# Second fold of the query weights as three products of f16 parts, with scales found by two more all-reduces over the partitions, and one inverse root for the first two norms

## The reference

```python
x = x + attn(layernorm(x)); x = x + ffn(layernorm(x))
# attn: 16 heads, low-rank queries, keys and values from one latent of 64
q = (h @ Wqa) @ Wqb                  # nope part 64, rope part 64 of each head
c_kv, k_pe = split(h @ Wkva, 64)     # latent 64, rope key 64
k_nope, v = split(c_kv @ Wkvb)       # 64 and 128 of each head
scores = [q_nope, rope(q_pe)] @ [k_nope, rope(k_pe)].T / sqrt(128), causal
attn_out = (softmax(scores) @ v) @ Wo
# ffn: router softmax over 16 experts, top 2, expert width 176, plus a shared expert of width 352
```

## Time and profile before

| | us |
|---|---|
| median of 3 runs | 1742.45 (1738.38 to 1745.92) |
| the profiled execution, its own time | 1731.52 |
| its span, first to last instruction | 1729.7 |
| PE busy | 1514.9 (88%) |
| DVE busy | 1314.3 (76%) |
| ACT busy | 1027.5 (59%) |
| POOL busy | 989.7 (57%) |
| start of the first scores of tile 0 | 79.6 |

### The profile page before, as it was taken

The page is one execution under the profiler, slowest core; times in us unless marked ns, Lnnn a source line. Parts: engine busy times, 40 slices in busy tenths (PEclk is TensorE's granted clock), DMA queues, the critical chain, the costliest instruction groups (busy, mean ns, idle before and its releaser), DMA issues.

```text
span 1729.7 us, 45005 instructions
## 1 busy us (share of the span) xinstructions
PE 1514.9 (88%) x16388; PEld 1089.9 (63%) x16389; DVE 1314.3 (76%) x2967; ACT 1027.5 (59%) x2342; POOL 989.7 (57%) x1597
## 2 busy tenths in 40 slices
PE   8777989889889999998899999988999999889990
PEld 2355666666656776666567766665677666666660
DVE  2587888888778778877887788778877888555556
ACT  1365656656656666666666666666666666556660
POOL 3156764435487676556876765568766443553440
PEclk9999999999999999999999999999999999999995
DMA  6236842221363333212634332126233311347418
GB/s 181 55 89 150 151 75 43 60 55 22 68 117 66 70 63 63 55 22 63 123 66 70 62 64 55 21 62 124 63 67 55 59 32 26 89 137 228 133 41 297
DMA packets 329877, 144.41 MB, mean 83 GB/s; under 512 B 277346, under 2 KB 320389, under 8 KB 329672
## 3 DMA queue, kind: packets, MB, share of 16 engines
q1 hardware_dynamic: 304592, 105.41, 30.5%
q10 hardware_dynamic: 18168, 19.41, 3.7%
q0 software_dynamic: 6912, 16.83, 3.1%
HBM read 47.04 MB, written 29.53 MB: 44 GB/s over the span
## 4 chain that ended last, share of the span: by engine, by line
PE 48%; DVE 26%; ACT 8%; issue 5%; DMA 5%; SPq 2%; POOL 1%; ACTq 0%; DVEq 0%; POOLq 0%
PE of_ps L681 20%; PE s_ps L681 16%; PE t_ps L842 10%; DVE pT L1613 7%; DVE smax L1584 3%; ACT pT L1028 3%; DVE smax L1588 2%; DVE nmax L1595 2%; DMA qT<-work 2%; DVE smax L1566 1%; ACT probs L1155 1%; DVE work L1418 1%; DVE nmax L1592 1%; ACT probs L1160 1%; ACT work L1028 1%
## 5 line engine op out<-in xcount | busy, mean ns | idle before, releaser
L1613 DVE TENSOR_TENSOR pT<-t_ps,pT 128x512 f16<-128x512 f32 (+3 forms) x688 | 409.5, 598 | 164.0 <-ACT pT L1028 160.6
L681 PE MATMUL s_ps<-kT,qT 128*128 128x512 f16 (+3 forms) x2304 | 492.3, 328 | 12.4 <-DMA qT<-work 7.7
L1028 ACT CAST pT<-t_ps 128x512 f16<-128x512 f32 (+3 forms) x688 | 354.5, 515 | 235.1 <-PE t_ps L842 234.5
L842 PE MATMUL t_ps<-id,probs 128*128 128x128 f32 x2304 | 381.3, 280 | 74.7 <-DVE pT L1613 34.7
L842 PEld LDWEIGHTS t_ps<-id,probs 128*128 128x128 f32 x2304 | 256.9, 141 | 178.5 <-issue 90.6
L1155 ACT ACTIVATE probs<-s_ps,nmax,fac 128x640 f32<-128x640 f32 (+3 forms) x256 | 269.0, 1051 | 1.7 <-DVE nmax L1592 1.7
L681 PEld LDWEIGHTS s_ps<-kT,qT 128*128 128x128 f16 x2304 | 219.0, 99 | 80.4 <-DMA qT<-work 8.3
L681 PEld LDWEIGHTS of_ps<-ckv,pT 128*128 128x128 f16 x6912 | 241.1, 98 | 38.8 <-DVE o_sb L1447 8.8
L681 PE MATMUL of_ps<-ckv,pT 128*128 128x64 f16 x6912 | 258.3, 193 | 6.5 <-DVE o_sb L1447 6.1
L681 PE MATMUL of_ps<-weights,xT 128*128 128x512 f16 (+1 forms) x936 | 200.2, 351 | 37.0 <-DVE ks_sb L1405 19.0
L1584 DVE TENSOR_REDUCE smax<-s_ps 128x1 f32<-128x512 f32 (+1 forms) x256 | 157.2, 647 | 3.6 <-PE s_ps L681 3.2
(11 more groups left out here) (224 smaller groups left out, 2444.7 us busy)
## 6 DMA issues: line engine op xcount, KB each, us to landing
wgu_sb<-wgu ACTq DMA_DIRECT2D x8, 704.0 KB, 4.4
work<-lists SPq DMA_DIRECT2D x40, 128.5 KB
qT<-lists SPq DMA_DIRECT2D x40, 128.5 KB, 2.1
x_sb<-x SPq DMA_DIRECT2D x32, 128.0 KB, 2.4
x<-x SPq DMA_DIRECT2D x32, 128.0 KB, 2.5
dense<-den SPq DMA_DIRECT2D x32, 128.0 KB, 2.1
weights<-dense ACTq DMA_DIRECT2D x1, 4096.0 KB, 20.0
qT<-y_exp SPq DMA_DIRECT2D x16, 256.0 KB, 6.8
```

Source lines behind the costliest of these rows:

```text
L681: return pe_.matmul(o, a, b, start=start, stop=stop)
L842: last = pe_.transpose(t_ps[:, h, c * P:(c + 1) * P], probs[:, u % 2, g * L + j * P:g * L + (j + 1) * P], id32[:, :])
L1028: return act.copy(o, i)
L1613: dve.tensor_tensor(pT[:, u % 2, 1, h, 0:w], t_ps[:, h, 0:w], pT[:, u % 2, 0, h, 0:w], ALU.subtract).then_inc(s.lo_p, 1)
```

## The change

The second fold multiplies f16 parts of scaled operands. For that the scales of three operands are needed before it: of `Wqa` (A), of the rope columns (B) and of the first fold's product (C). DVE finds the largest magnitudes of A and B from the loaded weights (`fold_factors`) and of C from PSUM in two halves (`fold_products`); POOL reduces them over the partitions in two all-reduces (`fold_reduce`: A and B, then C); DVE makes the scales (`fold_scales`), ACT ten hi parts of at most 512 columns, DVE ten lo parts. Each part of the fold is then six f16 products, and the copy by ACT multiplies the scales back. The parts come in another order (both halves of the width for one column block, then the next), and the copy of C to SBUF as f32 falls away. The twelve small constant instructions of DVE move to between the two halves of this, and the means of the first two tiles come before them. On POOL the inverse roots of tiles 0 and 1 are made in one go of 14 steps; the wide instructions of both tiles come after the second `fold_reduce`; the all-reduce of `first_weights` comes before `norm` of tile 2 instead of behind it.

```diff
-            last.then_inc(s.qb_made, 1)
-            pe_.wait_ge(s.w_a, 16 * 4)
-            for m in range(KD):
-                for n, c in enumerate(WQ_ORDER):
...
-                    mm(s_ps[:, c, :], r_wqaT[:, 0, m * P:(m + 1) * P], src[:, 0, cc], True, False)
-                    mm(s_ps[:, c, :], r_wqaT[0:QLB, 1, m * P:(m + 1) * P], src[0:QLB, 1, cc], False,
-                       True).then_inc(s.wq_made, 1)
+                if h % 4 == 3:
+                    last.then_inc(s.qb_made, 1)
+
+            for n, (m, c) in enumerate(WQ_PARTS):
+                right, cc = (f_qb, c * 512) if c < 2 else (f_pe, (c - 2) * 512)
+                pe_.wait_ge(s.fold_lo, 4 + 2 * (n // KD))
+                if n >= 4:
+                    pe_.wait_ge(s.wq_copied, n - 3)
+                for k, r in CHUNKS:
+                    for a, b in ((0, 0), (0, 1), (1, 0)):
+                        last = mm(s_ps[:, n % 4, :], f_wqa[0:r, a, k, m * P:(m + 1) * P], right[0:r, b, k, cc:cc + 512],
+                                  k + a + b == 0, k == 1 and a == 1)
+                last.then_inc(s.wq_made, 1)
...
+            act.wait_ge(s.fold_scaled, 1)
+            fold_hi(0, 6)
+            folded(0, 3)
+            act.wait_ge(s.fold_scaled, 2)
+            fold_hi(6, 10)
+            folded(3, 8)
...
+            def fold_scales(first, last, n):
+                cols = slice(first, last)
+                dve.wait_ge(s.fold_reduced, n + 1)
+                link(dve.tensor_scalar(fold_all[:, cols], fold_all[:, cols], 1e-30, None, ALU.max))
+                link(dve.tensor_scalar(fold_amp[:, cols], fold_all[:, cols], 1.0 / WMAX, None, ALU.mult))
+                dve.tensor_tensor(fold_f[:, n:n + 1], fold_amp[:, 0:1], fold_amp[:, n + 1:n + 2], ALU.mult)
+                link(dve.reciprocal(fold_inv[:, cols], fold_amp[:, cols]))
+                dve.sem_inc(s.fold_scaled, 1)
+
+            def fold_factors():
+                link(dve.memset(fold_max[:, :], 0.0))
+                dve.wait_ge(s.w_a, 16 * 4)
+                for k, r in CHUNKS:
+                    largest(fold_max[0:r, k:k + 1], r_wqaT[0:r, k, :])
+                    last = largest(fold_max[0:r, 2 + k:3 + k], r_pe[0:r, k, :])
+                link(last)
+                link(largest(fold_top[:, 0:2], fold_max[:, 0:4].rearrange("p (a b) -> p a b", b=2)))
+                dve.sem_inc(s.fold_found, 1)
+
+            def fold_products(g):
+                dve.wait_ge(s.qb_made, g + 1)
+                largest(fold_max[:, 4 + 2 * g:5 + 2 * g], of_ps[:, g, :])
+                last = largest(fold_max[0:QLB, 5 + 2 * g:6 + 2 * g], t_ps[0:QLB, g, :])
+                link(last)
+                if g == 1:
+                    link(largest(fold_top[:, 2:3], fold_max[:, 4:8]))
+                    dve.sem_inc(s.fold_found, 1)
...
-            means(0, -1)
-            means(1, -1)
+            first_means()
+            fold_factors()
+            fold_products(0)
+            fold_scales(0, 2, 0)
+            fold_lo(0, 6)
+            fold_products(1)
+            constants()
+            fold_scales(2, 3, 1)
+            fold_lo(6, 10)
             means(2, -1)
             first_weights()
...
-            norm(pool, 0, -1)
-            norm(pool, 1, -1)
-            norm(pool, 2, -1)
+            def fold_reduce(first, last, n):
+                pool.wait_ge(s.fold_found, n + 1)
+                pool.partition_all_reduce(fold_all[:, first:last], fold_top[:, first:last], P,
+                                          bass.bass_isa.ReduceOp.max).then_inc(s.fold_reduced, 1)
+
+            fold_reduce(0, 2, 0)
+            inverse_root(pool, 0, 0, 2)
+            pool.sem_inc(s.ln_s, LN_STEPS)
+            fold_reduce(2, 3, 1)
+            scaled(pool, 0, 0, x_sb[:, 0, :], xs[:, 0:D], xs[:, D:2 * D], 0, s.ln1_done)
+            pool.wait_ge(s.xT_in, 16)
+            scaled(pool, 0, 1, x_sb[:, 1, :], xs[:, 0:D], xs[:, D:2 * D], 1, s.ln1_done)
+            pool.sem_inc(s.normed, 2)
             pool.wait_ge(s.amax_ready, 1)
             pool.partition_all_reduce(amax_all[:, 0:2], amax[:, 0:2], P, bass.bass_isa.ReduceOp.max).then_inc(s.amax_reduced, 1)
+            norm(pool, 2, -1)
```

More of the change, by code:

```diff
@@ L300, in build @@
         WQ_ORDER = (2, 3, 0, 1)
+        WQ_PARTS = [(m, c) for c in WQ_ORDER for m in range(KD)]
         SPLITS = [
@@ L635, in s_off, with inverse_root @@
             return g * (P if i == 0 else 2 * P if i == 1 else 512)
[L637 to L639 removed]
+        def inverse_root(eng, n, k0, k1):
             w = [ln_w[:, a, k0:k1] for a in range(3)]
@@ L651, in norm, with scaled @@
                 st_.do(eng.tensor_tensor(y, y, u, ALU.mult))
+        def scaled(eng, k, col, src, hi, lo, tile, done):
+            eng.tensor_scalar(xn[:, :], src, ln_mv[:, col, 0:1], ln_w[:, 1, col:col + 1], ALU.subtract, ALU.mult).then_inc(xn_s[k], 1)
+            eng.wait_ge(xn_s[k], tile + 1)
+            eng.tensor_copy(hi, xn[:, :]).then_inc(done, 1)
+            eng.wait_ge(done, 2 * tile + 1)
+            eng.tensor_tensor(lo, xn[:, :], hi, ALU.subtract).then_inc(done, 1)
+            eng.wait_ge(done, 2 * tile + 2)
+        def norm(eng, n, p, between=None):
+            inverse_root(eng, n, 0 if has(n) else 1, 2 if has(p) else 1)
             if between is not None:
@@ L1042, in _, with fold_hi, folded @@
             load(r_wr, gateT.rearrange("(k p) n -> p k n", p=P), s.w_b)
[L1045 to L1051, removed]
+            def fold_hi(first, last):
+                for raw, hi, lo, r, col in FOLD[first:last]:
+                    act.activation(hi, raw, ACT.Copy, scale=fold_inv[0:r, col:col + 1]).then_inc(s.fold_hi, 1)
+            def folded(first, last):
+                for n in range(first, last):
+                    m, c = WQ_PARTS[n]
+                    act.wait_ge(s.wq_made, n + 1)
+                    act.activation(r_wq[:, m, c * 512:(c + 1) * 512], s_ps[:, n % 4, :], ACT.Copy,
+                                   scale=fold_f[:, n // 4:n // 4 + 1]).then_inc(s.wq_copied, 1)
+            act.wait_ge(s.fold_scaled, 1)
[4 more added lines that the diff above has]
+            folded(3, 8)
             def hi_parts(splits):
@@ new lines, in fold_lo @@
+            def fold_lo(first, last):
+                for k in range(first, last):
+                    raw, hi, lo, r, col = FOLD[k]
+                    dve.wait_ge(s.fold_hi, k + 1)
+                    dve.scalar_tensor_tensor(lo, raw, fold_inv[0:r, col:col + 1], hi, ALU.mult, ALU.subtract).then_inc(s.fold_lo, 1)
+            def fold_factors():
[7 more added lines that the diff above has]
+                dve.sem_inc(s.fold_found, 1)
@@ L1477, in means, with first_means @@
                 last.then_inc(s.stats, 1)
+            def first_means():
+                for n in range(2):
+                    dve.wait_ge(xin[n], 16)
+                    last = dve.bn_stats(ln_st[:, n, 0:6], x_sb[:, n, :])
+                last.then_inc(s.stat_s, 2)
+                dve.wait_ge(s.stat_s, 2)
+                for n in range(2):
+                    last = dve.bn_aggr(ln_mv[:, n, :], ln_st[:, n, 0:6])
+                last.then_inc(s.stats, 2)
             def gate_hidden(q):
```

64 lines of the change are left out of this document (34 added, 30 removed).

## The result

| | before | after |
|---|---|---|
| median of 6 runs | 1744.18 us (1738.38 to 1746.5) | 1757.20 us (1752.37 to 1762.97) |
| ratio | | 1.0079, 95% interval 1.0054 to 1.0104 |
| profiled execution | 1731.52 us | 1757.62 us |
| start of `rope(0)` | 62.51 us | 75.91 us |

The ratio is 13.8 us of the median of before. The forecast was 1751.8 us in a range of 1735 to 1759, and 9.3 us for the shift of `rope(0)`; the chip took 13.4. The two profiled executions lie 26.1 us apart, more than the medians do, because the one of before lies 12.7 under its own median. So the start of `rope(0)` and the ratio are read, not the difference of those two.

What follows compares the result with a forecast made beforehand. PE's second f32 fold filled the start; after the change POOL's all-reduce switches would bound it, moving rope(0) from 62.51 to 71.8. The 9.3 us added to 1742.45 gave 1751.8 us, range 1735 to 1759.

Steps and rivals of the forecast that it cites:

- PE's gain: In the second fold, 32.1 us of f32 products removed, 48 f16 products added at 20.6 us, 2.6 a part.
- Steps 1 and 2: At the start, DVE's means and magnitude searches end at 18.4; POOL's first all-reduce runs from 18.55 to 18.9.
- Step 3: On POOL after the first all-reduce: 7.0 us back to ordinary instructions, then the shared root in 3.92 us.
- Step 4: On POOL: 6.0 us switch, second all-reduce, 6.0 back, tile 0 in 2.46, turn of xs 2.5, tile 1 in 2.46.
- Step 5: DVE's means of tile 2 and eight reductions before first_weights' all-reduce: 9.4 us covering POOL's switch; all-reduce at 59.0.
- Step 6: On POOL: third all-reduce, 6.0 us back, norm of tile 2 in 6.4, so rope(0) starts at 71.8.
- the price of a way back: x, POOL's cost from an all-reduce to ordinary instructions: 7.0 us at 18.9, 6.0 elsewhere; below x = 3.2 the kernel gains.
- A: POOL's return from an all-reduce is free (x = 0): 1735.6 us, or 1733.4 with a short switch; chance 0.20.
- B: POOL's switches cost 4 to 5.5 us; x = 5 gives +5.3 us, 1747.7 us; chance 0.20.
- C: Each POOL return costs 7.0 us, rope(0) +11.3; with POOL's steps slowed by DVE +14, 1756.5 us; chance 0.12.
- D: PE's new fold parts end late, needing to lose another 6 us; given no chance of its own.
- The yardstick: Start of rope(0) on POOL: its shift, forecast as 9.3 us later, passes whole to the kernel's end.

Runs made afterwards that it cites:

- Experiment 4: Changed kernel with the 64-row second chunk of the fold's f16 operands zero-filled to 128 rows; ratio to before 1.0078, rope(0) at 76.19 us.
- experiment 1: Changed kernel without its two new all-reduces, fold scales from a constant; ratio to before 1.0002, rope(0) at 62.81 us.
- Experiment 3: Kernel before plus one spare all-reduce of a constant on POOL between the norms of tiles 0 and 1; ratio to before 1.0024, rope(0) at 68.29 us.
- experiment 5: Changed kernel with all three early all-reduces replaced by PE and DVE exchanges, and two orders changed; ratio to before 0.9976, rope(0) at 62.25 us.
- experiment 2: Changed kernel with the second fold all-reduce directly behind the first, both ahead of the root; ratio to before 1.0034, rope(0) at 70.12 us.
- experiment 6: experiment 5's kernel with the fold's operands zero-filled to 128 rows; ratio to before 0.9943, rope(0) at 54.47 us.
- experiment 7: Kernel before with only the shared inverse root for tiles 0 and 1, fold still f32; ratio to before 1.0006, rope(0) at 62.76 us.
- experiment 8: experiment 1's kernel with norm of tile 2 moved ahead of first_weights' all-reduce; ratio to before 0.9975, rope(0) at 59.34 us.
- experiment 9: Kernel before with the f32 fold's second chunk zero-filled to 128 rows; ratio to before 0.9982, rope(0) at 55.26 us.

## Why the prediction came out as it did

The mechanism, the sign and every link of the chain were as forecast; the size of the shift was 4.1 us short. Of the 5.4 us between 1751.8 and 1757.2, another 1.7 come from the median of before, 1742.45 of three runs in the forecast and 1744.18 of six now. By the forecast's own steps:

- **PE's gain.** 24 products took 11.21 us, 2.8 a part for the forecast 2.6. Six spacings of 0.43 us and about 0.11 for each of two changes between 128 and 64 rows give 2.8; the second term was missing. So the fold was busy 22.4 us and ended at 51.9, where the prediction's signs said 13 to 21 and the forties. The clock stayed at the level of 1.2 GHz, as the spacing shows. PE was late for nobody, with 52 as the end of the last part and 56.2 as the start of the reductions. Experiment 4 shows that the clock didn't matter.
- **Steps 1 and 2.** First all-reduce at 18.25 (18.55 forecast).
- **Step 3, way back.** 8.59 for 7.0: +1.6. Root 3.88.
- **Step 4.** Switch 6.31 (6.0): +0.3. Way back 6.74 (6.0): +0.7. Turn of `xs` 2.78 (2.5): +0.3. Wide instructions as forecast.
- **Step 5.** From the end of tile 1 to the all-reduce 9.23 (9.35). Here the switch is hidden, as said.
- **Step 6.** Way back 6.87 (6.0): +0.9. `norm` of tile 2 6.94 (6.4): +0.6, 0.4 of it in its first step, 0.64 us for 0.25 before. Hand-over to `rope(0)` 0.27, counted at nothing: +0.3.

**The term that was mis-sized is the price of a way back**, taken as "7.0 for the way back at 18.9, where DMA is full, and 6.0 elsewhere". It was 8.6, 6.7 and 6.9: 3.2 of the 4.1 us. The reading of rows 9 as the switch ending last was right: at the same place the profiles of experiments 1, 3 and 5 name no releaser, with 7.3 to 7.6 us. The error was to take the clean 6.0 of the other direction for a lower price and give the 7.0 to DMA traffic. Ahead of `rope(0)`, over all runs, ways back took 6.7 to 8.6 us (ten bare ones, mean 7.3), bare switches to an all-reduce 5.9 to 6.3 (six, beside the 6.03 of rows 8). Experiment 3's way back came with no f16 part and no other edit beside it and still took 7.1. That only the one beside high DMA traffic (a share of 0.78 from 18 to 27 us) reached 8.6 may be contention, but in experiment 4 the same place took 7.7, so it isn't shown.

The Trainium skill (GPSIMD Engine Reference, section 2.1) gives about 6 us for the first call of a freshly loaded kernel. For the direction to the all-reduce the traces agree with 5.9 to 6.3. For the way back they show about 1 us more, and both prices were paid at every change of kind that no wait covered, not only at the first.

**The rivals.** A, a free way back, fell at once: at 27.22, 44.53 and 68.70 POOL waited 6.7 to 8.6 us for nothing else. B's x = 5 was too low. C had the better price, x = 7 everywhere (+11.3 to +14), and the result lies inside it. With x = 7.4, the mean of the three, its 52.8 + 3x gives 75.0, and the small terms above the rest. C's second reason, POOL slowed by DVE, can be no more than the 0.6 us of the last norm, and no run tests it. D stayed idle. That 1757.2 lies within the range is owed to C, which had a chance of 0.12: the range was drawn up to 1759 for it. The likeliest case had 1749 to 1755 and +8 to +11, and the result lies outside both. The break-even of x = 3.2 was not tried, as no way was found to make a way back cheaper; experiment 1 takes out two of the three and lands at break-even by that.

**The yardstick.** The shift of `rope(0)` and the measured change agree within 2 us in experiments 1, 2, 3, 4, 6, 7 and 8 and in the changed kernel (13.4 against 13.8). In experiment 5 the time gained 3.9 us more than `rope(0)`, in experiment 9 4.1 less. So it is good to 0.1%, sometimes only to 0.25%. It holds for medians and not for a pair of executions: the prediction's word that the shift is passed on whole is not what the two profiles show. Against before, the same step of POOL's norm lies 9 us later at 537 us (537.35 and 546.40), and a later step of POOL 17.3 us at 1444 (1444.19 and 1461.48). Where this drift comes from was not tried.

**What stays open.** The two profiled executions differ by 25.8 us of span, and only 13.4 of it lies ahead of `rope(0)`. About 5 us of the rest are at one place late in the kernel. POOL's timeline of the changed kernel there, and the windows of it:

```profile
1539.66 0.98 POOL L2074 DMA_INDIRECT y_exp<-probs,qT  x1 [0.30 <-issue]
1542.98 0.98 POOL L2074 DMA_INDIRECT y_exp<-probs,qT  x1 [2.33 <-ACT probs L1277]
...
1548.54 0.85 POOL L1980 TENSOR_TENSOR hs<-hid,hs 128x352 f16<-128x352 f32 x1 [3.08 <-ACT hs L1048]
```

```profile
1536.00:1543.00 7.00, 1.83 (x15) 0.89 (x12) 1.41 (x5) 2.55 (x6) 3.75 (x5) 0.95 0.31 104
1543.00:1550.00 7.00, 5.83 (x32) 3.88 (x33) 2.83 (x11) 2.19 (x5) 3.48 (x7) 0.57 0.06 20
```

PE is busy 1.8 of 7 us, with 5.15 us of it in one wait, and in the next window its granted clock is 0.57. The three `y_exp` at 1539.66, 1542.98 and 1549.55 take 9.9 us from the first start to the last. In the kernel before, the same three start at 1522.66, 1523.95 and 1527.43, 4.8 us. The profiled execution of experiment 9 has the same stop, its counterpart being 7 us with PE busy 1.3 and then a clock of 0.56; none of the other nine has one. It comes in executions of a kernel that starts late and of one that starts early, so it isn't put down to the change. What sets it off was not tried.

## What to carry to other kernels

Before a small cross-partition instruction is put between ordinary ones in GpSimd's queue, price the change of kind on both sides (here 5.9 to 6.3 us there and 6.7 to 8.6 back, against 0.4 for the instruction) and name the wait that hides it; where none does, group such calls or find the maximum with PE and DVE (1.4 to 1.8 us for one or two columns here). Before f32 products are split into f16 parts for speed, look at their spacing and why it is what it is: here half of them had half their rows empty, and filling these with zeros halved the block by itself, though the time of the whole showed at most a part of it. When one engine is relieved, follow the new chain through the idle ones: POOL is the least busy engine of the changed start (8.4 of 55 us) and is its bound, through time that counts as idle.

## What the runs showed of the hardware

- **With every other chunk on 64 rows, PE stayed at 1.2 GHz.** 32.1 us of f32 products and 22.4 us of f16 ones (experiment 1) ran back to back at the spacing of that level to the end. With 128 rows the spacing of the f16 products fell from 0.43 to 0.22 us at about 28 us in experiment 4, and that of the f32 records from 0.86 to 0.43 at about 23 in experiment 9. Filling the rows also takes away the short pauses at each change of rows; which of the two kept the clock down is not separated. The granted clock reads 1.00 in the windows of the slow streams and ahead of both rises, so the spacing has to be read. The Trainium skill (TensorE: Matmul & The Clock Gate, "What's actually happening") says that the default state is throttled and that activity releases it; the traces show that for full rows only.
- **A change in the number of rows costs PE about 0.11 us.** In the changed kernel two products of the same rows start 0.43 us apart, across a change it is 0.57, and 0.40 for the next; a part of six takes 2.79 us in place of 6 x 0.427.
- **A change of kind on POOL, bare, took 5.9 to 6.3 us to an all-reduce and 6.7 to 8.6 back.** It starts at the end of the instruction before it and runs under a wait for another engine, as under the 9.2 us ahead of the all-reduce at 61.45.
